# Causal attention on one core: the row maxima of two heads run in the two halves of TensorE's rows, the scores in three single PSUM banks, one exponential per head, 19 loads per unit

## The chip, the cores and the metric

The kernel runs on one NeuronCore of a Trainium2 chip. The metric is the device time in microseconds (us) of one execution of the whole program. PE is TensorE, PEld its weight loads, DVE VectorE, ACT ScalarE, POOL GpSimd, and SP (SPq for its queue) the engine that issues the transfers.

## The reference

The program is a chain of four layers on x of shape 8 x 1024 x 256, each of the form x = x + layernorm(f(layernorm(x))). The change touches the first, causal attention with 16 heads of width 16:

```python
c_q = x @ W_dq;   Q = (c_q @ W_uq).reshape(Bx, Sx, 16, 16)
c_kv = x @ W_dkv; K = (c_kv @ W_uk)...; V = (c_kv @ W_uv)...
scores = einsum('bqhd,bkhd->bhqk', Q, K) / sqrt(16)
attn = softmax(where(causal, scores, -inf), axis=-1)
out = einsum('bhqk,bkhd->bqhd', attn, V).reshape(Bx, Sx, 256) @ W_o
```

The layers behind it are a feed-forward layer with ternary weights, a linear attention that squares its scores (in this kernel the same function as the first, with other settings) and a ternary projection.

## The kernel before, in words

The passes run one after the other: weights, latent (norm, projections, Q, K and V to DRAM), attend with softmax (tiles named `a_`), mix, feed-forward, features, attend without softmax (tiles named `b_`), mix, ternary. Each pass has one program per engine, and every engine works its own program off in order.

**Operands.** Q and K are kept in fp32 accuracy as three bf16 parts each. A head has only 16 features, so `unit_operands` stacks six products of parts along the contraction: 96 rows (`STACK`), in which q holds parts 0,0,0,1,1,2 and k parts 0,1,2,0,1,0. Two more rows (96 and 97) hold minus the row maximum of the scores in two bf16 parts in q, and ones in k. A matmul over 98 rows so gives scores less their maximum. `set_rows` fills rows 96 to 127 once on POOL before the loads. Seven transfers load a unit: q and k for each of the three groups of parts (48, 32 and 16 rows of 8 KB), and v.

**Units.** A unit is 4 heads of one batch entry, 32 units in all. Operands of three units are held (`RING`); the tiles of the first are `first_q`, `first_k` and `first_v`, loaded during the latent pass. Unit n has ten steps: pieces of 512 columns of transposed scores (keys on the partitions), 4608 columns a head. In step s, PE computes for the four heads the scores of step s + 2 (`scores`, line 993), which ACT turns into weights (line 896), POOL masks on the diagonal (line 869), and `weigh` (line 1009) multiplies with v in fp32, four heads side by side in four groups of 32 columns of the array.

**Maxima.** Row maxima are needed before the scores, one unit ahead. PE computes the same scores the other way round (queries on the partitions, `maximum_scores`, line 982) in 36 chunks of 512 columns per unit, each in one PSUM bank; DVE reduces each chunk (line 945 whole, or line 947 with the causal mask). After the last chunk `largest` (lines 953 to 961) turns the maxima into rows, and SP copies them with 8 transfers into the q tile (line 818). In unit n, chunks 16 to 35 of unit n + 1 and then chunks 0 to 15 of unit n + 2 are computed; the first of unit n + 2 waits until all its operands are loaded.

**PSUM.** There are eight banks: 0 to 3 for scores, as two pairs; one exponential of 128 x 1024 covers the two heads of a pair. Banks 4 to 6 take maximum chunks, each free again when DVE has read it. Bank 7 takes the weighted sums.

**Order.** PE's order in a full step is written out: scores of heads 0 and 1, one chunk of maxima, scores of heads 2 and 3, two chunks, `weigh`, one chunk. In steps 2 and 9 (256 columns) it is one chunk after each pair of scores. SP's order in a unit: load of unit n + 2 (released when all weighing of unit n - 1 is done), store of half 0, the rows of maxima of unit n + 1, store of half 1.

Of the kernel before, what the change touches and what calls it, by code (L numbers as in the profile page):

```python
# [35 lines left out]
P = 128  # L36
# [4 lines left out]

STACK = 16 * 6


# [433 lines left out]
def latent_pass(nc, z, m, first):  # L478
    G, DC, GROUPS = z.G, z.DC, z.TILES // z.G
    with ExitStack() as ctx:  # L480
# [18 lines left out]
        @block.sync  # L499
        def _(sp):  # L500
            for u in range(2):
                sp.sem_inc(stored[u], STORED)

            def store(i, u):
                n = 2 * i + u
                sp.wait_ge(vx_ready, 2 * n + 3)
                for t in range(G):
                    sp.dma_start(m.v_dram[bass.ts(i, z.UPB), :, u * G + t, :].rearrange("g p k -> p g k"),
                                 vx[u][:, t, :, :].rearrange("p (g h) k -> p g (h k)", g=z.UPB)).then_inc(stored[u], 16)
                sp.wait_ge(low_done, n + 3)  # L510
# [6 lines left out]
            sp.wait_ge(first_set, 2)  # L517
            for dst, src in unit_operands(z, m, *first, 0):
# [4 lines left out]
            sp.wait_ge(first_loaded, 16 * 7)  # L523
            for u in range(2):
                sp.wait_ge(stored[u], STORED * (GROUPS // 2 + 1))
# [160 lines left out]
def unit_operands(z, m, q_tile, k_tile, v_tile, n):  # L686

    width = z.HPU * z.S
    q, k = [tile[:, :, :].rearrange("p h t -> p (h t)") for tile in (q_tile, k_tile)]
    parts = [m.qk_dram[:, which, bass.ts(n, z.HPU * z.DK), :].rearrange("g (d h) t -> d g (h t)", h=z.HPU)  # L690
             for which in range(2)]
    pairs, row = [], 0
    for q_part, groups in ((0, 3), (1, 2), (2, 1)):
        into = slice(row, row + z.DK * groups)
        q_rows = parts[0][:, q_part:q_part + 1, :]
        pairs.append((q[into, :], q_rows.to_broadcast([z.DK, groups, width]) if groups > 1 else q_rows))
        pairs.append((k[into, :], parts[1][:, 0:groups, :]))
        row += z.DK * groups
    pairs.append((v_tile[:, :, :], m.v_dram[bass.ts(n, 1), :, :, :].rearrange("n p k c -> p (n k) c")))
    return pairs  # L700
# [4 lines left out]
def attend_pass(nc, z, m, first, softmax):  # L705
# [5 lines left out]
    RING = 3  # L711
# [16 lines left out]
    AHEAD = 2  # L728
    PAIRS = 2 if softmax else 3
    SLOTS = 5  # L730
    assert STEPS % SLOTS == 0 and 2 * RING * STEPS % PAIRS == 0

# [11 lines left out]
    assert sum(map(sum, MOST)) == CH  # L744
    with ExitStack() as ctx:
# [15 lines left out]
        st_ready, p_ready, masked, pv_done, o_taken = sm("st_ready", "p_ready", "masked", "pv_done", "o_taken")  # L761
        LOADED = 16 * 7
        STORED = 16
        SB, OB = 4, (7 if softmax else 6, 7)
        OT = len(set(OB))
        PV, PR, STK, DR = SLOTS, PAIRS, SRING, 2
        if softmax:
# [15 lines left out]

        OPERAND = slice(0, STACK + 2 if softmax else STACK)

# [4 lines left out]
        def score_bank(r, s, hd):  # L790
            return 2 * ((2 * (STEPS * r + s) + hd // 2) % PAIRS) + hd % 2

# [9 lines left out]
        def _(sp):  # L802
# [3 lines left out]
            def load(n, r):  # L806
                if softmax:
                    sp.wait_ge(rows_set, 2 * n if isinstance(n, int) and n < RING else 2 * (RING - 1))
                pairs = unit_operands(z, m, qs[r], ks[r], vs[r], n)
                for dst, src in pairs:  # L810
                    sp.dma_start(dst, src).then_inc(loaded[r], 16)

            def load_rows(n, r):
                sp.wait_ge(rows_ready, n + 1)
                for k in range(2):
                    at = qs[r][STACK + k:STACK + k + 1, :, :].rearrange("o h (q b i) -> o (h q) b i", b=4, i=32)
                    for b in range(4):
                        sp.dma_start(at[:, :, b, :], rows[32 * b:32 * b + 32, k, :]).then_inc(rows_loaded, 16)
# [28 lines left out]
        def _(pool):  # L847
# [5 lines left out]
            if first:  # L853
                pool.wait_ge(bias_ready, 1)
                for r in range(1, RING):
                    set_rows(pool, qs[r], ks[r], rows_set, 2 * (r - 1))

            def unit(n, r, rnd, ahead, far):
                for s in range(STEPS):
                    if not DIAG[s]:  # L860
                        continue
                    if not softmax:
                        pool.wait_ge(d_ready, STEPS * n + s + 1 + DR)
                    wait_alone(pool, p_ready, 2 * STEPS * n + 2 * s + 2 + PR, m.alone)
                    for k, at in enumerate(DIAG[s]):
# [9 lines left out]
        def _(act):  # L875
# [13 lines left out]
            def weights(n, r, s):  # L889
                cols = slice(live_from(s), 512)  # L890
                act.wait_ge(pv_done, STEPS * n + s + 1)
                for k in range(2):
                    act.wait_ge(st_ready, 2 * STEPS * n + 2 * s + k + 1)
                    heads = 2 if softmax or k == 0 else 1
                    at = score_bank(r, s, 2 * k)
                    act.activation(p[s % SLOTS][:, 2 * k:2 * k + heads, cols], m.psum[:, at:at + heads, cols],  # L896
                                   ACT.Exp if softmax else ACT.Square, scale=z.DK ** -0.5).then_inc(p_ready, 1)
# [77 lines left out]
        def _(pe):  # L975
            pe.sem_inc(pv_done, PV)
            def maximum_scores(n, r, a, b):
                for c in range(a, b):
                    hd, pieces = chunks[c // 2][0] + c % 2 * HPU // 2, chunks[c // 2][1]
                    pe.wait_ge(s_taken, CH * n + c + 1)  # L980
                    for qt, h, at, w in pieces:
                        last = pe.matmul(m.bank[SB + c % SRING][:, at:at + w], qs[r][0:STACK, hd, qt * P:(qt + 1) * P],  # L982
                                         ks[r][0:STACK, hd, h * 512:h * 512 + w], start=True, stop=True)
                    last.then_inc(s_ready, 1)

            def scores(n, r, s, k):
                h, pieces = steps[s]
                pe.wait_ge(p_ready, 2 * STEPS * n + 2 * s + k + 1)
                if not softmax and k == 0:
                    pe.wait_ge(d_ready, STEPS * n + s + 1)  # L990
                for hd in (2 * k, 2 * k + 1):
                    for kt, at, q, w in pieces:
# [5 lines left out]
            def weigh(n, r, s):  # L998
                h, pieces = steps[s]
                pe.wait_ge(p_ready, 2 * STEPS * n + 2 * s + 2 + PR)  # L1000
                if not softmax:
# [17 lines left out]
            def unit(n, r, rnd, ahead, far):  # L1019
                def some_maxima(first, count):  # L1020

                    if not softmax:
                        return
                    late = CH - 2 * EARLY
                    for k in range(first, first + count):
                        if k < late and ahead:
                            maximum_scores(n + 1, (r + 1) % RING, 2 * EARLY + k, 2 * EARLY + k + 1)
                        if k >= late and far:
                            if k == late:
                                pe.wait_ge(loaded[(r + 2) % RING], LOADED * (rnd + (r + 2) // RING) + LOADED)  # L1030
                            maximum_scores(n + 2, (r + 2) % RING, k - late, k - late + 1)

                dealt = 0
                for s in range(STEPS):
# [4 lines left out]
                    at = (n, r, t) if t < STEPS else (n + 1, (r + 1) % RING, t - STEPS)  # L1039
                    for k in range(3):  # L1040
                        if k == 2:
                            weigh(n, r, s)
                        elif there:
                            scores(*at, k)
                        some_maxima(dealt, MOST[s][k])
                        dealt += MOST[s][k]

            if softmax:
                pe.wait_ge(loaded[0], LOADED)
                maximum_scores(0, 0, 0, CH)  # L1050
                pe.wait_ge(loaded[1], LOADED)
                maximum_scores(1, 1, 0, 2 * EARLY)
            operands(0, 0, 0)
            for s in range(AHEAD):
                for k in range(2):
                    scores(0, 0, s, k)
# [801 lines left out]
```

## Time and profile before

| | |
|---|---|
| median of 3 runs | 2884.16 us (2873.43 to 2885.13) |
| profiled execution | 2883.56 us |
| its span | 2881.8 us |
| PE busy | 2467.9 us, 86% |
| DVE busy | 2230.5 us, 77% |
| ACT busy | 1759.3 us, 61% |
| POOL busy | 562.9 us, 20% |
| mean granted clock of PE | 0.945 |

The span is the time from the first to the last instruction that the profile shows. Busy shares are means over all passes. Matmul records carry a start and a modelled end, so that neighbours overlap; the distance between starts is the safer reading.

### The profile page before, as it was taken

How to read it: one execution, taken by the hardware profiler on the slowest of the kernel's cores; microseconds unless marked ns; L12 is line 12 of the kernel's file. 1: busy time of each engine (PE TensorE's matmuls, PEld its weight loads, DVE VectorE, ACT ScalarE, POOL GpSimd, SP SyncE). 2: the span in 40 equal slices, each digit the busy share in tenths (PEclk: the TensorE clock that was granted, in tenths of full speed). 3: DMA queues.
4: the chain of work that ended last, by engine and by line, in shares of the span. 5: the costliest groups of instructions: out<-in, count | busy, mean ns of one | idle time of the engine just before them, and what ended most of it. 6: DMA issues, size and time to landing. Idle time of an engine off the chain costs nothing. (4 is left out here: it accounts for less than half of the span.)

```text
span 2881.8 us, 57144 instructions
## 1 busy us (share of the span) xinstructions
PE 2467.9 (86%) x15239; PEld 1169.6 (41%) x15239; DVE 2230.5 (77%) x5755; ACT 1759.3 (61%) x2682; POOL 562.9 (20%) x644
## 2 busy tenths in 40 slices
PE   3687999999999999677999997994899999996656
PEld 1342333333333333254666664552233333333544
DVE  4887889999899899286777767995566666666968
ACT  0442566666666666415777756883678778873446
POOL 0344111121111112140000000222222222222200
PEclk9897899999999999898999998997899999998879
DMA  5497353545445353260000002556777777754403
GB/s 173 151 282 209 71 104 80 110 84 100 92 91 101 82 110 77 79 184 1 0 0 0 0 0 69 181 181 175 146 143 145 146 146 146 146 117 132 127 0 117
DMA packets 223820, 309.47 MB, mean 107 GB/s; under 512 B 32321, under 2 KB 170257, under 8 KB 211473
## 3 DMA queue, kind: packets, MB, share of 16 engines
q1 hardware_dynamic: 223472, 307.47, 44.3%
q10 hardware_dynamic: 288, 1.31, 0.3%
q8 instruction: 25, 0.41, 0.1%
q14 instruction: 35, 0.28, 0.0%
HBM read 181.29 MB, written 126.88 MB: 107 GB/s over the span
## 5 line engine op out<-in xcount | busy, mean ns | idle before, releaser
L896 ACT ACTIVATE a_p<-psum 128x1024 f32<-128x1024 f32 (+1 forms) x640 | 567.4, 941 | 305.5 <-PE psum L993 305.3
L896 ACT ACTIVATE b_p<-psum 128x512 f32<-128x512 f32 (+2 forms) x640 | 444.1, 749 | 157.5 <-PE psum L993 154.5
L947 DVE CUSTOM_DVE_ANT_0 a_dump<-psum,a_bias 128x128 bf16<-128x128 f32 (+3 forms) x1024 | 447.7, 488 | 62.3 <-PE psum L982 52.5
L945 DVE TENSOR_REDUCE a_peak<-psum 128x1 f32<-128x512 f32 x512 | 334.3, 687 | 23.1 <-PE psum L982 19.8
L993 PE MATMUL psum<-b_qs,b_ks 96*128 96x512 bf16 (+3 forms) x1536 | 307.2, 330 | 40.9 <-DMA b_vs<-values 40.9
L924 DVE COPY b_twin<-psum 128x512 f32<-128x512 f32 (+1 forms) x320 | 203.9, 637 | 177.0 <-PE psum L993 173.6
L1009 PE MATMUL psum<-b_p,b_vs 128*32 128x512 f32 (+3 forms) x3072 | 314.7, 497 | 6.3 <-POOL b_p L869 6.3
L869 POOL TENSOR_SCALAR_AFFINE_SELECT a_p<-a_p 128x512 f32<-128x512 f32 x256 | 162.5, 635 | 755.4 <-ACT a_p L896 743.7
L982 PE MATMUL psum<-a_ks,a_qs 96*128 96x128 bf16 (+2 forms) x1008 | 275.5, 334 | 27.8 <-DMA a_vs<-values 20.2
L869 POOL TENSOR_SCALAR_AFFINE_SELECT b_p<-b_p 128x512 f32<-128x512 f32 x256 | 159.5, 635 | 453.3 <-DVE b_p L927 442.9
L993 PE MATMUL psum<-a_qs,a_ks 98*128 98x512 bf16 x1008 | 234.4, 328 | 9.1 <-issue 3.6
L993 PEld LDWEIGHTS psum<-b_qs,b_ks 96*128 96x128 bf16 x1536 | 115.1, 98 | 303.4 <-issue 168.8
L927 DVE SCALAR_TENSOR_TENSOR b_p<-psum,b_twin 128x512 f32<-128x512 f32 (+1 forms) x320 | 204.3, 639 | 33.3
L1465 PE MATMUL psum<-f_xt,w_fc 128*128 128x512 f32 x512 | 224.9, 597 | 3.3 <-ACT f_hid L1406 2.8
L1009 PE MATMUL psum<-a_p,a_vs 128*32 128x512 f32 x2016 | 205.8, 496 | 0.5 <-POOL a_p L869 0.3
L1604 POOL TENSOR_TENSOR g_parts<-g_rest,g_parts 128x2048 bf16<-128x2048 f32 x16 | 66.2, 4134 | 639.5 <-DVE g_parts L1592 639.5
L1267 PE MATMUL psum<-wo,m_att 128*128 128x256 f32 x512 | 136.3, 427 | 62.3 <-POOL m_att L1214 39.4
L982 PEld LDWEIGHTS psum<-a_ks,a_qs 96*128 96x128 bf16 x1008 | 84.7, 97 | 224.6 <-DVE a_peak L947 118.1
L982 PE MATMUL psum<-first_k,first_q 96*128 96x128 bf16 (+3 forms) x528 | 150.1, 344 | 25.1 <-SPq L834 12.2
L1476 PE MATMUL psum<-w_proj,f_parts 128*128 128x256 bf16 x1536 | 170.3, 273 | 1.4 <-DVE f_scaled L1354 1.4
L1476 PEld LDWEIGHTS psum<-w_proj,f_parts 128*128 128x128 bf16 x1536 | 150.2, 98 | 19.4 <-DVE f_scaled L1354 1.7
L1343 DVE TENSOR_TENSOR f_rest<-f_sq,f_parts 128x512 f32<-128x512 f32 x128 | 88.5, 691 | 76.9 <-ACT f_sq L1414 75.8
(197 smaller groups left out, 3693.1 us busy)
## 6 DMA issues: line engine op xcount, KB each, us to landing
qk_parts<-l_parts SPq DMA_DIRECT2D x96, 256.0 KB, 3.1
qk_parts<-g_parts SPq DMA_DIRECT2D x96, 256.0 KB, 2.8
values<-l_vx SPq DMA_DIRECT2D x64, 256.0 KB, 3.3
sums<-a_osb SPq DMA_DIRECT2D x64, 256.0 KB, 2.1
m_num<-sums SPq DMA_DIRECT2D x64, 256.0 KB, 3.8
m_inv<-reciprocals SPq DMA_DIRECT2D x64, 256.0 KB, 4.4
values<-g_vx SPq DMA_DIRECT2D x64, 256.0 KB, 3.0
sums<-b_osb SPq DMA_DIRECT2D x64, 256.0 KB, 2.1
```

Of the source, the lines that this page charges most:

```text
L869: pool.affine_select(out=diag, in_=diag, compare_op=ALU.is_ge, fill=0.0, base=0, pattern=[[0, HPU], [1, P]], channel_multiplier=-1).then_i ...
L896: act.activation(p[s % SLOTS][:, 2 * k:2 * k + heads, cols], m.psum[:, at:at + heads, cols], ACT.Exp if softmax else ACT.Square, scale=z.D ...
L924: dve.tensor_copy(twin[s % 2][:, cols], bank).then_inc(twin_ready, 1)
L927: dve.scalar_tensor_tensor(out=p[s % SLOTS][:, 3, cols], in0=bank, scalar=1.0 / z.DK, in1=twin[s % 2][:, cols], op0=ALU.mult, op1=ALU.mult ...
L945: last = dve.tensor_reduce(dst, piece, AX.X, ALU.max)
L947: last = dve.tensor_tensor_reduce(dump[c % SRING][:, at:at + w], piece, bias[:, 512 - w:], 1.0, NEG, ALU.add, ALU.max, dst)
L982: last = pe.matmul(m.bank[SB + c % SRING][:, at:at + w], qs[r][0:STACK, hd, qt * P:(qt + 1) * P], ks[r][0:STACK, hd, h * 512:h * 512 + w], ...
L993: last = pe.matmul(m.bank[score_bank(r, s, hd)][:, at:at + w], ks[r][OPERAND, hd, kt * P:(kt + 1) * P], qs[r][OPERAND, hd, h * 512 + q:h * ...
L1009: last = pe.matmul(m.bank[OB[h]][32 * hd:32 * hd + 32, q:q + w], vs[r][:, kt, 32 * hd:32 * hd + 32], p[s % SLOTS][:, hd, at:at + w], start ...
L1267: last = pe.matmul(bank, att[u][:, c, t * P:(t + 1) * P], wo[:, c, :], start=(c == 0), stop=(c == DC - 1))
L1465: last = pe.matmul(m.bank[F0 + j % 4], m.w_fc[:, c, j * P:(j + 1) * P], xt[u][:, c, :], start=(c == 0), stop=(c == DC - 1))
L1476: last = pe.matmul(bank, parts[u][:, part, j, t * P:(t + 1) * P], m.w_proj[:, j, :], start=(part == j == 0), stop=(part == PARTS - 1 and j ...
```

## The change

- Loads: heads 0 and 1 (the first half of each tile) and heads 2 and 3 (the second half) are loaded apart, in 4 KB rows, 8 + 10 + 1 = 19 transfers per unit. The first half lies on rows 0 to 95, the second on rows 16 to 111 in another order of the products. The rows of minus the maximum move to 112 and 113, and scores run over 114 rows. POOL sets rows 0 to 31 of the second half too: four fills per tile pair where there were two. `first` is loaded in the latent pass in the same 19 transfers.
- Maxima: a head's maximum is taken from four of the six products (for the second half three and a remainder on rows 64 to 111). A head of the first half uses rows 0 to 63 of the array, one of the second rows 64 to 111. For each piece a matmul of one and a matmul of the other follow each other, into two banks. A pair waits until both its banks are read. There are four banks (3 to 6) for maxima.
- Scores: one bank a head, three in all (0 to 2), and one exponential of 128 x 512 per head, 40 per unit where there were 20.
- Order of PE in a full step: scores 0, a pair of maxima, scores 1, `weigh`, a pair, scores 2, scores 3. In steps 2 and 9 the second pair is left out.

```diff
+MAIN = 16 * 4
+TOP = 16 * 7
...
+            for dst, src in unit_operands(z, m, *first, 0, 2, True):
...
+    low, second = slice(0, MAIN // 2), slice(q.shape[1] // 2, q.shape[1])
...
+    eng.memset(q[low, second, :], 0.0).then_inc(step, 1)
+    eng.wait_ge(step, done + 3)
+    eng.memset(k[low, second, :], 1.0).then_inc(step, 1)
...
+LOWER = ((0, 0, 3), (1, 0, 1), (1, 1, 1), (2, 0, 1))
+UPPER = ((2, 0, 1), (1, 1, 1), (0, 2, 1), (0, 0, 2), (1, 0, 1))
...
+        row = TOP - STACK if apart and half else 0
+        for q_part, k_part, groups in (LOWER, UPPER)[half] if apart else SHARED:
+            into = slice(row, row + z.DK * groups)
+            q_rows = parts[0][:, q_part:q_part + 1, :]
+            pairs.append((q[into, :], q_rows.to_broadcast([z.DK, groups, heads * z.S]) if groups > 1 else q_rows))
+            pairs.append((k[into, :], parts[1][:, k_part:k_part + groups, :]))
+            row += z.DK * groups
...
-    PAIRS = 2 if softmax else 3
+    WIDE = 1 if softmax else 2
+    PER = HPU // WIDE
+    SCORES = 3
...
-    SRING = 3
+    SRING = 4
...
-    MOST = [(1, 1, 0) if s in LAST else (1, 2, 1) for s in range(STEPS)]
+    MOST = [(1, 0) if s in LAST else (1, 1) for s in range(STEPS)]
...
+                for j in range(a, b):
+                    hd, pieces = chunks[j]
+                    pe.wait_ge(s_taken, CH * n + 2 * j + 2)
                     for qt, h, at, w in pieces:
+                        for half, rows_of in enumerate((slice(0, MAIN), slice(MAIN, TOP))):
+                            last = pe.matmul(m.bank[SB + (2 * j + half) % SRING][:, at:at + w],
+                                             qs[r][rows_of, hd + 2 * half, qt * P:(qt + 1) * P],
+                                             ks[r][rows_of, hd + 2 * half, h * 512:h * 512 + w], start=True, stop=True)
...
+                    if there:
+                        scores(*at, 0)
+                    some_maxima(dealt)
+                    if there:
+                        scores(*at, 1)
+                    weigh(n, r, s)
+                    if MOST[s][1]:
+                        some_maxima(dealt + 1)
+                    for k in (2, 3):
+                        if there:
                             scores(*at, k)
```

The attend pass without softmax keeps its pairs of banks, its seven loads and its order.

## Rows read from the trace of the kernel before

**Rows 1.** Busy time of each engine in one stretch of the softmax attend pass

```profile
600.00:800.00 200.00, 188.45 (x1359) 69.15 (x1357) 181.01 (x600) 131.11 (x156) 36.21 (x57) 1.00 0.47 96
```

**Rows 2.** Timeline of PE in one unit: start, length, what, count

```profile
701.14 0.39 PE L982 MATMUL psum<-first_k,first_q 96*128 96x128 bf16 x2
...
703.99 0.39 PE L982 MATMUL psum<-first_k,first_q 96*128 96x256 bf16 x2
...
704.65 0.38 PE L982 MATMUL psum<-first_k,first_q 96*128 96x512 bf16 x1
704.87 0.59 PE L993 MATMUL psum<-a_qs,a_ks 98*128 98x512 bf16 x2
705.30 0.38 PE L982 MATMUL psum<-first_k,first_q 96*128 96x512 bf16 x1
705.62 0.64 PE L1009 MATMUL psum<-a_p,a_vs 128*32 128x256 f32 x8
706.19 0.60 PE L993 MATMUL psum<-a_qs,a_ks 98*128 98x512 bf16 x2
...
712.97 0.38 PE L982 MATMUL psum<-first_k,first_q 96*128 96x512 bf16 x1
714.15 0.39 PE L982 MATMUL psum<-a_ks,a_qs 96*128 96x128 bf16 x2 [0.80 <-DMA a_vs<-values]
```

**Rows 3.** Groups of DVE by shape, 263 to 1165 us, all 32 units

```profile
L945 DVE TENSOR_REDUCE a_peak<-psum 128x1 f32<-128x512 f32 x512 | 334.3, 687 | 23.1 <-PE psum L982 19.8
L947 DVE CUSTOM_DVE_ANT_0 a_dump<-psum,a_bias 128x512 bf16<-128x512 f32 x256 | 169.5, 689 | 20.9 <-PE psum L982 20.7
L947 DVE CUSTOM_DVE_ANT_0 a_dump<-psum,a_bias 128x384 bf16<-128x384 f32 x256 | 141.5, 553 | 0.0
L947 DVE CUSTOM_DVE_ANT_0 a_dump<-psum,a_bias 128x256 bf16<-128x256 f32 x256 | 97.9, 421 | 8.0 <-PE psum L982 5.3
...
L947 DVE CUSTOM_DVE_ANT_0 a_dump<-psum,a_bias 128x128 bf16<-128x128 f32 x256 | 73.8, 288 | 33.4 <-PE psum L982 26.5 <-POOL a_bias L851 1.0
```

**Rows 4.** Timeline of DVE around the end of a unit's maxima

```profile
686.24 0.22 DVE L953 TENSOR_REDUCE a_npeak<-a_peak 128x32 f32<-128x64 f32 x1
...
687.65 0.29 DVE L947 CUSTOM_DVE_ANT_0 a_dump<-psum,a_bias 128x128 bf16<-128x128 f32 x1
...
714.27 0.22 DVE L953 TENSOR_REDUCE a_npeak<-a_peak 128x32 f32<-128x64 f32 x1
```

**Rows 5.** Waits, 600 to 800 us: us in total, times, longest

```profile
PEld psum L982 <- DVE a_peak L947: 38.3, 56, 2.1
...
DVE a_dump L947 <- PE psum L982: 10.3, 29, 0.7
...
PE psum L982 <- DMA a_vs<-values: 4.6, 4, 1.6
```

**Rows 6.** Groups by shape, 600 to 800 us: ACT's 128 x 512

```profile
L896 ACT ACTIVATE a_p<-psum 128x512 f32<-128x512 f32 x28 | 15.3, 609 | 5.4 <-PE psum L993 5.4
```

**Rows 7.** Timeline of ACT: two pair exponentials back to back

```profile
704.85 1.94 ACT L896 ACTIVATE a_p<-psum 128x1024 f32<-128x1024 f32 x2 [0.91 <-PE psum L993]
```

**Rows 8.** Timeline of SP: first two and last two of a unit's loads

```profile
700.69 0.63 SPq L811 DMA_DIRECT2D a_qs<-qk_parts  x1
701.51 0.61 SPq L811 DMA_DIRECT2D a_ks<-qk_parts  x1
...
704.25 0.37 SPq L811 DMA_DIRECT2D a_ks<-qk_parts  x1
704.81 0.35 SPq L811 DMA_DIRECT2D a_vs<-values  x1
```

**Rows 9.** Transfers by line: count, KB each, median us from issue to landing

```profile
sums<-a_osb SPq DMA_DIRECT2D x64, 256.0 KB, 2.1
```

**Rows 10.** Line 682 on POOL: ns shortest, median and longest, first and last start

```profile
L682 POOL MEMSET a_ks<- x2: 3506/3506/3506, 267.3 to 274.5; 32x4096 bf16 x2
```

**Rows 11.** Timeline of ACT in the latent pass, behind the load of `first`

```profile
161.91 2.06 ACT L595 ACTIVATE l_parts<-psum 128x512 bf16<-128x512 f32 x4 [4.96 <-DMA qk_parts<-l_parts]
```

More of the change, by code:

```diff
@@ L516, in _ @@
                 sp.wait_ge(stored[u], STORED * 2)
-            sp.wait_ge(first_set, 2)
-            for dst, src in unit_operands(z, m, *first, 0):
+            sp.wait_ge(first_set, 4)
+            for dst, src in unit_operands(z, m, *first, 0, 2, True):
                 sp.dma_start(dst, src).then_inc(first_loaded, 16)
@@ L683, in set_rows, with unit_operands @@
     eng.wait_ge(step, done + 2)
[L686 to L698, printed above, removed]
+    eng.memset(q[low, second, :], 0.0).then_inc(step, 1)
+    eng.wait_ge(step, done + 3)
+    eng.memset(k[low, second, :], 1.0).then_inc(step, 1)
+    eng.wait_ge(step, done + 4)
+SHARED = ((0, 0, 3), (1, 0, 2), (2, 0, 1))
+LOWER = ((0, 0, 3), (1, 0, 1), (1, 1, 1), (2, 0, 1))
+UPPER = ((2, 0, 1), (1, 1, 1), (0, 2, 1), (0, 0, 2), (1, 0, 1))
+def unit_operands(z, m, q_tile, k_tile, v_tile, n, halves=1, apart=False):
+    heads = z.HPU // halves
+    pairs = []
+    for half in range(halves):
+        q, k = [tile[:, half * heads:(half + 1) * heads, :].rearrange("p h t -> p (h t)") for tile in (q_tile, k_tile)]
+        parts = [m.qk_dram[:, which, bass.ts(n, z.HPU * z.DK), :].rearrange("g (d x h) t -> d g x (h t)", x=halves,
+                                                                         h=heads)[:, :, half, :] for which in range(2)]
+        row = TOP - STACK if apart and half else 0
[5 more added lines that the diff above has]
+            row += z.DK * groups
     pairs.append((v_tile[:, :, :], m.v_dram[bass.ts(n, 1), :, :, :].rearrange("n p k c -> p (n k) c")))
@@ L807, in load @@
                 if softmax:
-                    sp.wait_ge(rows_set, 2 * n if isinstance(n, int) and n < RING else 2 * (RING - 1))
-                pairs = unit_operands(z, m, qs[r], ks[r], vs[r], n)
+                    sp.wait_ge(rows_set, 4 * n if isinstance(n, int) and n < RING else 4 * (RING - 1))
+                pairs = unit_operands(z, m, qs[r], ks[r], vs[r], n, *((2, True) if softmax else ()))
                 for dst, src in pairs:
@@ L863, in unit @@
                         pool.wait_ge(d_ready, STEPS * n + s + 1 + DR)
[L864 removed]
+                    wait_alone(pool, p_ready, PER * STEPS * n + PER * s + PER + PR, m.alone)
                     for k, at in enumerate(DIAG[s]):
@@ L891, in weights @@
                 act.wait_ge(pv_done, STEPS * n + s + 1)
[L892 to L896, printed above, removed]
+                for k in range(PER):
+                    act.wait_ge(st_ready, PER * STEPS * n + PER * s + k + 1)
+                    heads = WIDE if softmax or k == 0 else 1
+                    at = score_bank(r, s, WIDE * k)
+                    act.activation(p[s % SLOTS][:, WIDE * k:WIDE * k + heads, cols], m.psum[:, at:at + heads, cols],
                                    ACT.Exp if softmax else ACT.Square, scale=z.DK ** -0.5).then_inc(p_ready, 1)
@@ L1019, in unit, with some_maxima @@
             def unit(n, r, rnd, ahead, far):
[L1020 to L1031, printed above, removed]
+                def some_maxima(j):
+                    late = CP - EARLY
+                    if j < late and ahead:
+                        maximum_scores(n + 1, (r + 1) % RING, EARLY + j, EARLY + j + 1)
+                    if j >= late and far:
+                        if j == late:
+                            pe.wait_ge(loaded[(r + 2) % RING], LOADED * (rnd + (r + 2) // RING) + LOADED)
+                        maximum_scores(n + 2, (r + 2) % RING, j - late, j - late + 1)
                 dealt = 0
@@ L1039, in unit @@
                     at = (n, r, t) if t < STEPS else (n + 1, (r + 1) % RING, t - STEPS)
[L1040 to L1043, printed above, removed]
+                    if not softmax:
+                        for k in range(PER):
+                            if there:
+                                scores(*at, k)
+                        weigh(n, r, s)
+                        continue
+                    if there:
[3 more added lines that the diff above has]
+                        scores(*at, 1)
+                    weigh(n, r, s)
+                    if MOST[s][1]:
+                        some_maxima(dealt + 1)
+                    for k in (2, 3):
+                        if there:
                             scores(*at, k)
-                        some_maxima(dealt, MOST[s][k])
-                        dealt += MOST[s][k]
+                    dealt += sum(MOST[s])
             if softmax:
                 pe.wait_ge(loaded[0], LOADED)
-                maximum_scores(0, 0, 0, CH)
+                maximum_scores(0, 0, 0, CP)
                 pe.wait_ge(loaded[1], LOADED)
-                maximum_scores(1, 1, 0, 2 * EARLY)
+                maximum_scores(1, 1, 0, EARLY)
             operands(0, 0, 0)
             for s in range(AHEAD):
-                for k in range(2):
+                for k in range(PER):
                     scores(0, 0, s, k)
```

34 lines of the change are left out of this document (15 added, 19 removed).

## The prediction, made before the changed kernel ran

> **What bounds the kernel now.** I read the page first: PE is busy for 86% of the span, DVE for 77%, ACT for 61%. These are means over nine passes, so I cut out the pass that the change touches. In 200 us of it PE is busy for 188.45 us, DVE for 181.01, ACT for 131.11, at a granted clock of 1.00 (2.4 GHz) and a DMA share of 0.47 [rows 1]. Two engines are nearly full there, and modelled ends make a busy PE look fuller than it is, so I went on by starts. In the timeline of PE [rows 2] one chunk of maxima takes 0.22 us from start to start (704.65 to 704.87), a full step 2.85 us (701.14 to 703.99), with no gap inside: scores, maxima and weighing follow each other. The reader is to see that PE is dense, and that its density is made of three equal parts: 4608 columns x 4 heads each for maxima and scores, and the weighing, whose four heads run side by side but pass four times.
>
> Then DVE. From the starts of the same kind in the timeline a whole chunk costs about 0.65 us, the masked pieces some 0.08 us less than their durations of 0.689, 0.553, 0.421 and 0.288 [rows 3]: 16 x 0.65 + 8 x (0.61 + 0.475 + 0.345 + 0.21) = 23.5 us a unit. The end of a unit's maxima costs 1.4 us more (686.24 to 687.65) [rows 4], and I add 0.5 us for the end of the loop, an estimate: about 25.4 us. The period of a unit is 714.27 - 686.24 = 28.03 us [rows 4]. So PE has to wait a little for DVE (38.3 us of weight loads held in seven units, most of it behind running matmuls, so hidden), DVE a little for PE (10.3 us), and once a unit PE waits for the last load: 4 times 4.6 us together [rows 5], and in the timeline 714.15 - 712.97 - 0.22 = 0.96 us [rows 2]. PE's own work is then about 28.03 - 0.96 = 27.1 us, of which about 1.2 us is short waits for DVE: 25.9 us packed.
>
> **The change part by part, for one unit of 28.03 us.**
>
> *Maxima side by side.* A matmul of a first-half head on rows 0 to 63 and one of a second-half head on rows 64 to 111 go to different banks. If they run together, half of 18,432 columns goes: 9,216 x 0.215/512 = 3.9 us off PE. The nearest row is the weighing, where eight instructions of 256 columns, in four column groups, take 0.57 us and not four times that (705.62 to 706.19) [rows 2]; but those are column groups. Bounds: 0 (they run one after the other) and -3.9. I take -3.9, since the weighing is the row that it is nearest to.
>
> *Changes of the array's shape.* From a maximum chunk into the weighing the start comes 0.32 us later (705.30 to 705.62) where 0.22 is usual: 0.10 us. Out of it, 0.57 us for 256 columns at four passes of 0.107 leave 0.14 us [rows 2]. Before there are 2 such changes a step, 20 a unit. After, with maxima in half rows, the order scores, maxima, scores, weighing, maxima, scores has 5 in a full step and 4 in steps 2 and 9: 48. That is 28 more. Bounds: 0 (a change of rows may cost nothing; no row shows one) and 28 x 0.14 = 3.9 us, which eats the whole gain. I take 0.10, the entry: +2.8 us. The Trainium skill says it of tiling in general (TensorEngine Tiling (Array Packing), Key Properties): changing the tiling mode, not merely the tile, drains the engine. It gives no price; by that rule the lower bound of 0 falls away, by the rows both ends stay open, and this is the rule that speaks against the change.
>
> *Scores in single banks.* Bank k is free when the exponential of three scores earlier has ended. The critical one is scores 1, which waits for scores 2, three before it: matmul 0.38, exponential 0.609 [rows 6], two handovers of about 0.05, so 1.09 us. The way of PE between them is 3 x 0.215 + 0.22 + 2 x 0.10 = 1.07 us. They meet; I put +0.1 us a unit. If the changes are free, the way is 0.87 and this wait gives back 0.2 us of each full step, 1.6 us a unit: a cheap change is then worth less.
>
> *Forty exponentials.* Two of 128 x 1024 back to back take 1.94 us, so 0.92 each from start to start; four halves start every 0.48 us at best (0.609 less the same overlap), 0.08 us more a step, and at worst 4 x 0.609 = 2.44 [rows 6, 7]. ACT goes from some 17.5 to 18.4 us, at worst 24, of 28: hidden under PE. If that cover goes, it is the bound only below 24 us.
>
> *19 loads.* SP issues the 48-row transfers 0.82 us apart and the 16-row ones 0.56 (704.25 to 704.81) [rows 8]. Two of 48 rows, fourteen of 16 and two of 32 (between, 0.7) take 1.6 + 7.8 + 1.4 = 10.8 us before v is issued, where it is 4.1 us now (700.69 to 704.81). But v now lands at 714.1, 13.4 us after the first issue, so it waits behind 1.5 MB. A transfer of 256 KB that stands alone lands in 2.1 us [rows 9]; 512 KB behind little then takes 3 to 4 us, which gives 13.8 to 14.8 us. PE asks later than now, behind the weighing of step 5: 5 steps of about 2.7 and one of 1.5, less 0.85, is 14.2 us after the unit's start, with the first issue 1.3 us after it. Wait 0.9 to 1.9 us where it was 0.96: bounds 0 and +1.0, I take +0.1, because SP's rate (64 KB in 0.56 us) is below what the engines move and leaves no queue. The eight row transfers and the stores stand behind 11 us of issue, with the rows wanted 14 us after the start: covered.
>
> *DVE.* Its work stays 25.4 us. A pair of banks is released together, so DVE has between one and two pairs (1.3 to 2.5 us) in hand, about as now. With PE at 25.9 - 3.9 + 2.8 + 0.1 = 24.9 us both are equal, and each delay of one shows at the other. The short waits were 1.2 us at 25.9 against 25.4; I take 1.2 + 0.3.
>
> Sum: -3.9 + 2.8 + 0.1 + 0.1 + 0.3 = -0.6 us; without the loss to the meeting of both, -0.9. I take -0.8 us for each of the 30 units with maxima beside them: -24 us.
>
> *Ahead of the units.* POOL fills 3.5 us more per tile pair (two halves of 3.506 us) [rows 10]; in the latent pass POOL is idle then, at the start of attend the load of unit 1 begins 3.5 us later, and its 19 issues add up to 3. DVE works on the 36 chunks of unit 0 meanwhile: +0 to 5, I take 2. In the latent pass SP's issues of `first` hold its stores 6.7 us longer. ACT already waits 4.96 us for a store behind that load [rows 11]; the queues drain while SP issues, so +0 to 7, I take 2. Together +4.
>
> Forecast: 2883.6 - 24 + 4 = 2863.6, say 2862 us. The profiled execution is 0.6 us under the median, so that the two are the same base. A difference of 0.5% (14.4 us) is about what a measurement of this kernel can tell from none.
>
> **The rivals.**
>
> *Changes are nearly free, DVE bounds.* PE falls to 22.1 us plus 1.6 for the exponentials; DVE's 25.4 us with 1 us of friction gives 26.4 a unit: -1.6 x 30 + 4 = -44, 2840 us. For it: both switches in the rows also change the data type and the column groups, a change of rows alone may be less. Against: the drain is that of the array itself.
>
> *The load holds the unit.* If 4 KB rows move no faster and v lands 16 us after the first issue, PE waits 3 us in each unit, 2 more than now: -0.8 + 2 - 0.6 (DVE's waits fall into it) = +0.6, so 2883.6 + 18 + 4 = 2906 us. It decides from 15.4 us of landing on. Against: issue, not bandwidth, sets the pace.
>
> *The two halves do not overlap.* PE keeps 25.9, gains 2.8 us of changes: 28.8 with its waits at least 29.8 a unit, +1.8 x 30 + 4: 2940 us. It decides when less than 0.8 of 3.9 us overlaps. For it: no row has two row groups at work. By the Trainium skill (TensorE: Matmul & The Clock Gate, Part 3) matmuls in distinct row groups run concurrently; no run here shows that yet.
>
> *The gain just covers the costs.* Changes at 0.13 us and load at its upper bound: within 15 us of before, 2880 us.
>
> **How the numbers follow.** Forecast 0.38 (2848 to 2874), free changes 0.24, costs cover the gain 0.18, load 0.10, no overlap 0.10. Faster by over 0.5% (under 2869.7): three quarters of the first and the second, 0.53, and a little of the last but two, 0.55; within: 0.22; slower: 0.23. The range 2828 to 2908 leaves out the no-overlap case, and some at each end.
>
> **What would show it.** In PE's timeline of the changed kernel: two maximum matmuls starting a few ns apart, the next 0.22 us on (right) or each 0.22 us (wrong); starts from scores 0 into a maximum chunk 0.32 us apart, or 0.22; a wait of scores 1 for ACT; the period between two starts of line 953's counterpart, forecast 27.2 us; the wait on v at half of each unit near 1 us. In the latent pass the wait of ACT for its store, 5 to 7 us. The forecast is wrong if the period stays near 28, or falls to 26.4.

## The result, and the profile after

The changed kernel takes 2898.16 us in the median of 7 runs (2891.59 to 2904.92), the kernel before beside it 2885.04 us (2870.02 to 2888.19). The ratio is 1.0057, interval 1.0033 to 1.0081: slower by 13 us. I had forecast 2862 us, a gain of some 22 us. The profiled execution took 2904.92 us.

The same stretch of the softmax attend pass as [rows 1], of the kernel after (columns: length, busy of PE, PEld, DVE, ACT, POOL, granted clock, DMA share, GB/s):

```profile
600.00:800.00 200.00, 181.30 (x1370) 53.91 (x1366) 172.78 (x599) 140.86 (x298) 35.53 (x56) 1.00 0.47 95
```

PE and DVE are both less busy than before (188.45 and 181.01) and neither is full: both wait more than before. The clock is the same. The unit is only 0.2 us longer (below), so DVE's smaller share is mostly less work: between 400 and 1050 us DVE is busy for 25.4 us a unit before and 24.4 after. Whole chunks that come as a pair start 0.60 us apart where 0.65 was usual, and the end of a unit's maxima takes 1.04 us where it took 1.4. That last difference comes from one operation (line 957, now 973): 0.55 us before, while a mask of POOL runs beside it, and 0.19 after, when POOL stands still.

The timeline of PE in one unit of the kernel after (start, length, what, count):

```profile
722.56 0.39 PE L999 MATMUL psum<-first_k,first_q 64*128 64x512 bf16 x2
722.88 0.39 PE L1012 MATMUL psum<-a_qs,a_ks 114*128 114x512 bf16 x1
723.20 1.06 PE L1028 MATMUL psum<-a_p,a_vs 128*32 128x512 f32 x8
724.97 0.39 PE L999 MATMUL psum<-a_ks,a_qs 64*128 64x128 bf16 x4 [0.70 <-DMA a_vs<-values]
...
731.87 0.39 PE L1012 MATMUL psum<-first_q,first_k 114*128 114x512 bf16 x1 [0.84 <-DMA first_q<-a_rows]
...
733.84 0.39 PE L999 MATMUL psum<-a_ks,a_qs 64*128 64x512 bf16 x2
734.16 0.82 PE L1012 MATMUL psum<-first_q,first_k 114*128 114x512 bf16 x4
734.91 0.39 PE L999 MATMUL psum<-a_ks,a_qs 64*128 64x512 bf16 x2
735.24 0.39 PE L1012 MATMUL psum<-first_q,first_k 114*128 114x384 bf16 x2
735.56 0.64 PE L1028 MATMUL psum<-a_p,a_vs 128*32 128x256 f32 x8
736.13 0.86 PE L1012 MATMUL psum<-first_q,first_k 114*128 114x384 bf16 x5
736.92 0.39 PE L999 MATMUL psum<-a_ks,a_qs 64*128 64x512 bf16 x2
737.24 0.28 PE L1012 MATMUL psum<-first_q,first_k 114*128 114x256 bf16 x1
738.19 1.07 PE L1028 MATMUL psum<-a_p,first_v 128*32 128x512 f32 x8 [0.66 <-ACT a_osb L903]
```

Three things stand in it against [rows 2]. Two maximum matmuls of 512 columns (x2) are over in 0.39 us, the length of one, and the scores follow 0.32 us after their start: a pair costs what one cost, plus 0.10 us. That 0.10 us stands at each change of the array's shape (733.84 to 734.16, 722.88 to 723.20). And there are waits: 0.66 us of the weighing for ACT's copy of the sums, which was not there before, and 0.84 us of the first scores of a unit for the rows of the maxima, which was 0.3 us at most.

The waits of the kernel after, 600 to 800 us, beside [rows 5]:

```profile
PEld psum L999 <- DVE a_peak L963: 39.9, 46, 2.1
...
DVE a_dump L963 <- PE psum L999: 15.2, 24, 1.0
PEld psum L1028 <- ACT a_osb L903: 11.1, 14, 0.9
...
DVE a_peak L961 <- PE psum L999: 10.0, 25, 0.6
PE psum L1028 <- ACT a_osb L903: 7.7, 14, 0.7
...
PE psum L999 <- DMA a_vs<-values: 3.8, 4, 1.2
...
PE psum L1012 <- DMA a_qs<-a_rows: 2.3, 3, 0.9
```

The wait on `a_osb` comes 14 times in seven units, twice a unit. From the starts it is 738.19 - 737.24 - 0.21 = 0.74 us before a unit's first weighing, and 0.51 us before its fourth: 1.25 us.

ACT at the first of these places, in the kernel after:

```profile
734.59 3.06 ACT L912 ACTIVATE a_p<-psum 128x512 f32<-128x512 f32 x6 [1.05 <-PE psum L1012]
737.53 0.60 ACT L903 ACTIVATE a_osb<-psum 128x512 f32<-128x512 f32 x1
738.01 0.68 ACT L912 ACTIVATE a_p<-psum 128x256 f32<-128x256 f32 x2
```

The last weighing of the unit is over at 736.13, when PE goes on to scores 2. The copy stands in ACT's program behind the four exponentials of that step, and scores 2 and 3 of the step are now issued behind the weighing. So ACT can't copy before it has had scores 2 and 3: 737.53, where behind the weighing alone it could start at about 736.2 (an estimate from the weighing's end). Bank 7 is the only one for sums, and the next weighing (738.19) needs it. Before, all four scores of a step stood ahead of the weighing, and the copy was next for ACT when the weighing ended.

The period of a unit by DVE's last operation on the maxima (first and last start; before, then after in a fence of its own):

```profile
L961 DVE STREAM_TRANSPOSE a_rows<-a_split x24: 245/245/246, 405.2 to 1053.4; 128x64 bf16<-128x64 bf16 x24
```

```profile
L977 DVE STREAM_TRANSPOSE a_rows<-a_split x23: 245/245/246, 411.9 to 1036.3; 128x64 bf16<-128x64 bf16 x23
```

(1053.4 - 405.2) / 23 = 28.18 us before, (1036.3 - 411.9) / 22 = 28.38 us after. These are means. In both profiles the granted clock falls to its lower level, 0.50 (1.2 GHz), for 3.4 us in two of the thirty units, and such a unit takes 29.5 to 29.7 us; in the changed kernel it does so for 6.8 us in one more, which takes 32.1 us. The median unit is 28.03 us before and 28.27 after.

**Where the 14 us are.** In the two profiles the last instruction on a tile of the softmax attend pass starts at 1196.9 and 1211.3 us: +14.4, about the whole difference of the medians (13.1). 2.9 us come ahead of the pass (first maximum matmul at 263.1 and 266.0), 9.6 us in the thirty units with maxima (845.0 and 854.6 us from the second unit's rows to the last; 30 x 0.24 = 7 us by the median units, the rest is the clock), 2.3 us behind them, and 0.4 us are won between the first maxima and the second unit's rows. The 7 us by which the profiled execution is slower beyond that stand in the mix pass, whose code is the same, and the medians don't show them.

### The profile page after: what moved, and what is told of

It reads as the page before. It is cut to its first block and busy times, and to the rows that moved or that the text cites. A ratio compares the mean times of both kernels' runs of the same rounds, so it can differ in the third digit from the quotient of the medians.

```text
span 2903.2 us, 59404 instructions
## 1 busy us (share of the span) xinstructions
PE 2424.2 (83%) x15239; PEld 1097.5 (38%) x15239; DVE 2206.8 (76%) x5755; ACT 1806.5 (62%) x3322; POOL 572.6 (20%) x650
## 5 line engine op out<-in xcount | busy, mean ns | idle before, releaser
L912 ACT ACTIVATE a_p<-psum 128x512 f32<-128x512 f32 (+1 forms) x1280 | 614.4, 560 | 269.5 <-PE psum L1012 268.1
L963 DVE CUSTOM_DVE_ANT_0 a_dump<-psum,a_bias 128x128 bf16<-128x128 f32 (+3 forms) x1024 | 437.5, 486 | 82.2 <-PE psum L999 79.7
L961 DVE TENSOR_REDUCE a_peak<-psum 128x1 f32<-128x512 f32 x512 | 323.1, 684 | 44.8 <-PE psum L999 44.1
L1012 PE MATMUL psum<-a_qs,a_ks 114*128 114x512 bf16 x1008 | 246.6, 332 | 15.6 <-DMA a_qs<-a_rows 8.6
L999 PE MATMUL psum<-a_ks,a_qs 64*128 64x128 bf16 (+2 forms) x1008 | 150.6, 337 | 28.5 <-DMA a_vs<-values 23.6
L1294 PEld LDWEIGHTS psum<-wo,m_att 128*128 128x128 f32 x512 | 111.9, 223 | 95.8 <-DVE x L1202 36.2
L1492 PEld LDWEIGHTS psum<-f_xt,w_fc 128*128 128x128 f32 x512 | 97.2, 192 | 122.9 <-issue 112.7
```

Of the source, the lines that this page charges most:

```text
L912: act.activation(p[s % SLOTS][:, WIDE * k:WIDE * k + heads, cols], m.psum[:, at:at + heads, cols], ACT.Exp if softmax else ACT.Square, sca ...
L961: last = dve.tensor_reduce(dst, piece, AX.X, ALU.max)
L963: last = dve.tensor_tensor_reduce(dump[c % SRING][:, at:at + w], piece, bias[:, 512 - w:], 1.0, NEG, ALU.add, ALU.max, dst)
L999: last = pe.matmul(m.bank[SB + (2 * j + half) % SRING][:, at:at + w], qs[r][rows_of, hd + 2 * half, qt * P:(qt + 1) * P], ks[r][rows_of, h ...
L1012: last = pe.matmul(m.bank[score_bank(r, s, hd)][:, at:at + w], ks[r][OPERAND, hd, kt * P:(kt + 1) * P], qs[r][OPERAND, hd, h * 512 + q:h * ...
L1294: last = pe.matmul(bank, att[u][:, c, t * P:(t + 1) * P], wo[:, c, :], start=(c == 0), stop=(c == DC - 1))
```

## The experiments

Each ran beside the kernel before, whose medians there are 2880.5 to 2882.9 us (2885.04 beside the changed kernel); so two runs of this table are compared by their ratios as well as by their times. Times are medians; periods are means from the same line of DVE between 400 and 1060 us (28.18 us for the kernel before). By median units e1 is at 27.80 us, e4 at 28.28, e6 at 27.81: the clock is in the means of e4 and e6.

| run | time, us | ratio to before, interval | period, us |
|---|---|---|---|
| changed | 2898.16 | 1.0057, 1.0033 to 1.0081 | 28.38 |
| e1_sums_between | 2878.62 | 0.9997, 0.9982 to 1.0013 | 27.82 |
| e2_before_single_banks | 2944.26 | 1.0214, 1.0186 to 1.0242 | 30.05 |
| e3_before_split_loads | 2884.28 | 1.0003, 0.9986 to 1.0020 | 28.03 |
| e4_v_apart | 2895.40 | 1.0049, 1.0032 to 1.0066 | 28.50 |
| e5_ahead_9 | 2851.36 | 0.9880, 0.9849 to 0.9911 | 26.86 |
| e6_ahead_10 | 2888.87 | 1.0018, 1.0005 to 1.0030 | 28.07 |
| e7_before_v_apart_9 | 2851.31 | 0.9888, 0.9868 to 0.9908 | 27.17 |
| e8_ahead_7 | 2982.59 | 1.0355, 1.0333 to 1.0377 | 31.23 |
| e9_ahead_9_sums_last | 2875.81 | 0.9991, 0.9973 to 1.0008 | 27.72 |
| e10_pair_between_scores | 2858.90 | 0.9927, 0.9899 to 0.9955 | 27.11 |

**The sums between the exponentials.**

```diff
                 for k in range(PER):
+                    if k == PER // 2 and between:
+                        between()
                     act.wait_ge(st_ready, PER * STEPS * n + PER * s + k + 1)
...
-                    if s == LAST[0]:
-                        take_sums(n, 0)
-                take_sums(n, 1)
+                    sums = (lambda: take_sums(n, LAST.index(s))) if s in LAST else None
+                    inner = sums if softmax else None
```

> The changed kernel with one move in ACT's program: the copy of the weighted sums stands between the second and the third exponential of a step, not behind all four. First theory (the new wait of the weighing on that copy, 0.73 and 0.51 us a unit, is time of the unit): the period of a unit falls from 28.3-28.5 us to about 27.3, and the whole by 25 to 37 us. Rival (something else holds the unit, the maxima on DVE or the load, and takes the slack): the wait on the copy vanishes from the trace, the period stays within 0.3 us, the whole within 9 us.

2878.62 us: 19.5 us less than the changed kernel (17 by the ratios), and level with before. The wait on `a_osb` is gone from the list. The period fell by 0.56 us (0.47 by median units), between the two branches of the expectation and less than half of the 1.25 us that were freed. The waits of e1, 600 to 800 us:

```profile
PEld psum L1015 <- ACT a_p L914: 45.1, 120, 1.5
...
PE psum L1015 <- DMA a_qs<-a_rows: 5.6, 5, 1.3
```

The first scores of a unit wait longer for the rows of the maxima than in the changed kernel (2.3, 3 times), and the last load is waited for less (0.2 us a unit, by starts, where it was 1.0). The rest of the 1.25 us has a plainer answer in the trace. By starts (each distance between two starts of PE less the shortest that this pair of shapes shows) PE now waits 0.78 us a unit before scores 1, for ACT's exponential of scores 2, and it does so exactly twice a unit, in the steps in which the copy stands between the exponentials. One such place, in e5 (further below), which has the same order on ACT; first ACT, then PE:

```profile
716.47 0.63 ACT L906 ACTIVATE a_osb<-psum 128x512 f32<-128x512 f32 x1
716.95 2.12 ACT L917 ACTIVATE a_p<-psum 128x512 f32<-128x512 f32 x4
```

```profile
717.65 0.39 PE L1018 MATMUL psum<-first_q,first_k 114*128 114x512 bf16 x1 [0.27 <-ACT a_p L917]
```

The copy takes 0.48 us of ACT (716.47 to 716.95), the exponential of scores 2 comes so much later, and with three banks scores 1 needs its bank. So 1.25 us of waits became 0.78, a gain of 0.47, which is what the median unit fell by. One cause is shown, the place of the copy, and its size is enough for the loss of 13 us against before. It is not enough for the 36 us between forecast and result.

**Single banks alone, on the kernel before.** `WIDE = 1`, `SCORES = 3`, and the order kept: scores 0 and 1, a chunk, scores 2 and 3, two chunks, weighing.

> The kernel before with only one part of the change: scores in three single banks and one exponential a head; order of PE, maxima, loads as before. If the three single banks are dear by themselves (the ring: a score waits for the exponential three before it), each step waits about 0.2 us and the whole is 40 to 60 us slower. If they cost nothing by themselves (first theory: their cost in the changed kernel comes from the order, scores 2 and 3 behind the weighing), it is within 15 us of the kernel before.

2944.26 us, 63 us slower, 1.9 us a unit. In the old order scores 3 follow soon on scores 0, whose exponential they wait for. Its waits, 600 to 800 us:

```profile
PEld psum L995 <- ACT a_p L898: 40.4, 81, 0.8
...
PE psum L995 <- ACT a_p L898: 5.0, 14, 0.4
```

My first theory was wrong here: in the old order the three banks are dear by themselves. In the changed kernel they are not, and I put that down to scores 2 and 3 behind the weighing; no run has the new order without the other parts. The same order makes the copy of the sums late.

**Split loads alone, on the kernel before.** Each load by halves of the heads, both on rows 0 to 95: 13 transfers.

> The kernel before with the loads alone split by halves of the heads: 13 transfers a unit with rows of 4 KB in place of 7 with rows of 8 KB; all else as before. If the load of a unit is held by SP's rate of issue, v lands 1 to 2 us later, the wait of PE for v grows from about 1 to 2 or 3 us a unit, and the whole is 30 to 60 us slower. If bytes set it (first theory, since v's wait stayed at 1 us in the changed kernel), within 10 us of before, with up to 3 us lost in the latent pass.

No difference (2884.28 us). Rows of 4 KB in 13 transfers cost nothing in the units; the 19 of the change were not run alone. The waits for v even fell, from 20.9 to 6.4 us between 400 and 1050 us, and the median unit stayed at 28.0 us: in the kernel before that wait was not what held the unit.

**v on a semaphore of its own.**

```diff
-        LOADED = 16 * (19 if softmax else 7)
+        LOADED = 16 * (18 if softmax else 7)
+        v_loaded = sm(*[f"v_loaded{r}" for r in range(RING)])
...
+                    pe.wait_ge(v_loaded[r], 16 * rnd + 16)
                     pe.wait_ge(rows_loaded, ROWS_LOADED * n + ROWS_LOADED)
```

> The changed kernel with v counted on a semaphore of its own, for which PE waits only before the unit's first scores: the maxima two units ahead no longer wait for v. If the wait for v (about 1 us a unit) is on the path, the period falls by 0.5 to 1 us and the whole by 15 to 30 us; if DVE is then not ready either, the wait turns into one for DVE and the whole falls by under 9 us.

2895.40 us, its interval overlaps that of the changed kernel. The wait for v is gone, and the wait for the rows took its place: 29.3 us between 400 and 1050 us (two rows of the list, 20.4 and 8.9) where the changed kernel has 9.5 (6.3 and 3.2). Neither branch of the expectation named that, and it gave the next theory.

**A ring through the maxima.** In the unit of the changed kernel above: the first scores of a unit at 703.59, as at 731.87 a period later; the last pair of the next unit's maxima at 722.56; then, in the timelines of DVE and of SP's queue:

```profile
724.56 0.22 DVE L969 TENSOR_REDUCE a_npeak<-a_peak 128x32 f32<-128x64 f32 x1
725.33 0.24 DVE L977 STREAM_TRANSPOSE a_rows<-a_split 128x64 bf16<-128x64 bf16 x1
```

```profile
725.60 4.99 SPq L834 DMA_DIRECT2D first_q<-a_rows  x8
```

and the scores at 731.87. PE 18.97 us, DVE 3.04, transfers 6.27: together 28.28 us, the unit. Three stretches between four points always add up; what makes a ring of them is that each waits for the one before. The rows are issued as soon as DVE has them, the last of the eight lands 6.1 us after the first is issued, and the scores start 0.12 us behind that. DVE is not idle before the last pair either: it is still reading the pair before it, for which it had waited 0.23 us. In the kernel before the same points are these (PE, SP's queue, PE), with the last chunk at 712.97 [rows 2]:

```profile
693.91 0.60 PE L993 MATMUL psum<-a_qs,a_ks 98*128 98x512 bf16 x2
```

```profile
715.68 4.99 SPq L818 DMA_DIRECT2D first_q<-a_rows  x8
```

```profile
721.95 0.60 PE L993 MATMUL psum<-first_q,first_k 98*128 98x512 bf16 x2 [0.30 <-DMA first_q<-a_rows]
```

PE 19.06 us, DVE 2.71, transfers 6.27. The wait for v lies between the last maxima and the scores, beside DVE and the transfers and not in front of them; that is why e3 and e4 gained nothing when it shrank. To shorten the ring, the last maxima of a unit must be computed earlier in the unit before: `EARLY`, the pairs done two units ahead, was 8.

> The changed kernel with the sums between the exponentials, v on its own semaphore, and 9 in place of 8 pairs of maxima computed two units ahead, so that a unit's last pair of maxima, and with it the transfer of the maxima, comes one pair earlier. Theory: the ring last pair of maxima, DVE's end work, eight row transfers (7 us from their first issue to landing), scores of the next unit, holds the unit at 27.8 us. Then the period falls by up to one slot, 1.0 to 1.4 us, until DVE's 25.4 us or the load hold it: 26.6 to 27.2 us, the whole 2845 to 2862 us, and PE's wait for the rows falls from 1.2 us a unit to under 0.4. Rival (DVE or PE holds it, or the operands of two units ahead are not there yet): the wait for the rows turns into one for q and k or for DVE, the whole stays within 9 us of 2878.

> As the one before with 10 pairs two units ahead. If the ring of the rows held it with 9 too, another 0.5 us a unit; if the load of q and k has become late (asked for 2.4 us earlier than with 8), PE waits for it and the period goes back up by about 1 us, 30 us in the whole.

> The kernel before with v on its own semaphore and 9 (18 chunks) in place of 8 (16 chunks) two units ahead. The ring, worked out from its rows, is 28.1 us long there too. If it holds the kernel before as well, the period falls from 28.17 us to about 27.3 (PE's packed 25.9 us and its waits for DVE stop it there), the whole by 20 to 30 us. If PE alone holds it, it stays within 9 us of before.

> The changed kernel with the sums between the exponentials and 7 in place of 8 pairs two units ahead: the rows come one pair later. If the ring of the rows holds the unit, the period grows by 1.0 to 1.4 us and the whole by 30 to 42 us over 2878. If the load or DVE holds it, the wait for the load (0.2 us a unit there) goes and the whole stays or falls a little.

With 9: 2851.36 us, the period 26.86, and the rows are not in the list of waits. What is left there, 600 to 800 us:

```profile
PEld psum L1018 <- ACT a_p L917: 38.8, 124, 0.7
PEld psum L1005 <- DVE a_peak L969: 30.2, 49, 1.4
...
PE psum L1005 <- DMA a_ks<-qk_parts: 2.4, 4, 0.9
```

With 10 PE asks for q and k before they are there: 37.2 us of waits on them between 400 and 1050 us (25.3 and 11.9; with 9 it was 11.5), period 28.07, as expected. With 7 the period is 31.23, more than the one slot that I gave it: 3.4 us where 1.0 to 1.4 were expected. Its list and its stretch:

```profile
PE psum L1015 <- DMA a_qs<-a_rows: 12.4, 5, 2.5
```

```profile
600.00:800.00 200.00, 171.95 (x1219) 49.95 (x1218) 157.91 (x543) 126.32 (x264) 33.00 (x52) 0.94 0.38 79
```

PE stands still for up to 2.5 us a unit, and the granted clock of the stretch is 0.94, between its two levels of 1.2 and 2.4 GHz, where it was 1.00. Right behind that wait, in every unit, it stands at the lower level for 3.4 us (6.8 in every seventh or so):

```profile
702.40:705.80 3.40, 3.40 (x24) 0.94 (x23) 1.47 (x8) 1.19 (x2) 0.00 (x0) 0.51 0.00 0
```

In the kernel before a unit with one such stretch is 1.7 us longer than one without (29.7 and 28.0). That leaves some 1.7 us of the 3.4 for the slot, an estimate, against 1.0 to 1.4 expected. The direction and the place are those of the ring.

The kernel before with the same two edits takes 2851.31 us: the ring held it too. The two edits were not run apart there, but v's wait alone is ruled out by e3. The changed kernel, with its copy moved, is no faster than the kernel before when both have them (2851.36 and 2851.31 us). The period of the kernel before, 27.17 us, stands 1.3 us over the 25.9 us of PE's packed work, and the changed kernel's 26.86 us 2.0 us over 24.9 us.

**The fourth field.** Ring relaxed (v apart, 9), sums behind all exponentials as the change has them.

> The changed kernel with v apart and 9 pairs two units ahead, but ACT's copy of the sums behind all four exponentials as the change has it. It fills the fourth field beside the changed kernel (period 28.4), the one with the sums between (27.8) and the one with both (26.86). If the wait for the sums (1.25 us a unit) adds to whatever else holds the unit: period 26.86 + 0.6 to 1.25 = 27.5 to 28.1 us, the whole 2870 to 2888 us. If it counts only while the ring of the maxima's rows holds the unit: within 9 us of 2851.

2875.81 us: the copy's place costs 24 us also here (32 by the ratios; 0.86 us a unit). With the ring as it was it cost 19.5 us (17). So the waits of the weighing lie on the path in both cases: they are inside PE's part of the ring, and inside PE's own sum where the ring is relaxed.

**The second pair between scores 2 and 3**, on e5:

```diff
                     weigh(n, r, s)
-                    if MOST[s][1]:
-                        some_maxima(dealt + 1)
-                    for k in (2, 3):
-                        if there:
-                            scores(*at, k)
+                    if there:
+                        scores(*at, 2)
+                    if MOST[s][1]:
+                        some_maxima(dealt + 1)
+                    if there:
+                        scores(*at, 3)
```

> As the run with 9 ahead and the sums between (2851 us), with the second pair of maxima between scores 2 and scores 3 in place of ahead of both. One more change of the array's shape in a full step, 8 a unit at 0.10 us: +0.8 us. PE has then 1.5 us in place of 1.07 between scores 2 and the scores 1 that wait for its exponential, so that the wait there (0.86 us a unit in the run before) goes. If both are time of the unit they cancel: within 9 us of 2851. If the wait there was hidden behind DVE, the whole is 20 to 30 us slower; if the change of shape costs nothing, 20 us faster.

2858.90 us, 7.5 us over e5 by the times and 14 by the ratios (intervals 0.9899 to 0.9955 and 0.9849 to 0.9911, which just overlap), 0.25 us a unit: about the band of "they cancel". But half of the reason given for it did not happen. By starts PE's packed work (waits left out) is 25.7 us a unit where e5 has 24.9: the eight changes cost their 0.8 us. The wait before scores 1 did not go: it is still there twice a unit, 0.58 us where it was 0.78, at the copy again. The rest of what the changes cost was won at other waits.

## Why the prediction was wrong, by its own steps

- **Maxima side by side, -3.9 us: right.** Two matmuls in the length of one. The rival without overlap falls.
- **Changes of the array's shape, +2.8 us: right.** 0.10 us each (0.32 against 0.22), the value taken. The rival with free changes falls; the Trainium skill's rule that a changed tiling mode drains the engine (TensorEngine Tiling (Array Packing), Key Properties) agrees with these rows.
- **Packed work of PE, 24.9 us: right.** Through all starts between 400 and 1050 us, waits left out, the changed kernel has 28.38 - 3.5 = 24.9 us a unit, the kernel before 28.18 - 2.3 = 25.9.
- **Scores in single banks, +0.1 us: near in this order.** Between a pair and scores 1 the starts show 0.11 us a unit, and scores 3 wait another 0.13 us in each of the two short steps. But e2 shows 1.9 us in the old order, and in e1 and e5 the wait before scores 1 is 0.8 us. The prediction's sum for it (exponential and handovers against PE's way) has no copy in it, and the copy is what makes this wait.
- **19 loads: right.** v is issued 10.0 us after the first transfer (10.8 worked out) and PE has it 14.2 us after it (13.8 to 14.8). The rival in which the load holds the unit falls with that; that its 2906 us is the nearest of all to the result is chance, and so is a result inside the range, which reached so far up for its sake. The sentence behind it failed: that the eight row transfers are "covered". I put down when the rows are wanted and that SP is free, not when DVE has them. They land 0.12 us before the first scores start, in nearly every unit of both kernels.
- **Forty exponentials: the step that failed.** I costed them as ACT's busy time, "hidden under PE", and missed what moving scores 2 and 3 behind the weighing does to ACT's order: the copy of the sums comes after them, and one bank of sums makes PE wait 1.25 us a unit. Over thirty units that is about 37 us, the size of the miss of 36. Undoing it alone gives 17 to 19.5 us, because with three banks 0.78 of the 1.25 us comes back before scores 1.
- **DVE, +0.3 us: wrong in kind.** I took DVE's work as 25.4 us in both kernels and the 1.2 us of short waits as friction between two equal engines. DVE has 24.4 us in the changed kernel, and what held the unit was a ring of 28 us through PE, DVE and eight transfers. It gets shorter only by what falls in its parts. PE's part is 19.06 us before, 18.97 in the changed kernel with its copy late, and 18.50 in e1 (691.91 to 710.41); DVE's part, which ends on two chunks now where it ended on one, grew from 2.71 to 3.04 us and took 0.33 back. Of the gain of 1.0 us e1 so kept 0.23 by median units (0.36 by means). The ring is not the whole answer, though: with it relaxed for both, e5 against e7 keeps only 0.31.
- **Ahead of the units, +4 us: the size about right, the source wrong.** 2.9 us, in the latent pass. The prediction let POOL's two more fills cost nothing there. They are most of it. DVE's first operations of the pass (before, then after) end right behind POOL's fills (84.5 us before, 87.8 after), and the same four take 1.38 us when POOL stands still:

```profile
82.05 3.55 DVE L170 TENSOR_SCALAR l_xn<-x,l_mv,l_rs 128x256 f32<-128x256 f32 x4
```

```profile
81.62 6.68 DVE L172 TENSOR_SCALAR l_xn<-x,l_mv,l_rs 128x256 f32<-128x256 f32 x4
86.01 1.83 POOL L689 MEMSET first_k<- 32x2048 bf16 x1
91.88 1.38 DVE L172 TENSOR_SCALAR l_xn<-x,l_mv,l_rs 128x256 f32<-128x256 f32 x4
```

That is 3.1 us, and the load of `first` begins 2.5 us later (143.59 against 141.06). The load itself adds little: SP holds its stores for 10.3 us (143.59 to 153.85), 5.6 more than before, and ACT's wait behind it grew from 4.96 [rows 11] to 5.69 us:

```profile
165.15 2.06 ACT L597 ACTIVATE l_parts<-psum 128x512 bf16<-128x512 f32 x4 [5.69 <-DMA qk_parts<-l_parts]
```

The right sum: -1.0 us of packed work and +1.25 us for the copy, with the other waits as they were (2.3 us a unit before, 3.5 less 1.25 after), are +0.2 us a unit by the periods; over all thirty units of the two profiles it is 0.3 (9.6 us, some 2.5 of it the clock), and with 2.9 ahead, 2.3 behind and 0.4 won at the start the pass shows 14.4 us.

What stays open: e5 has 2.0 us of waits a unit over its packed work and e7 1.3. The 0.8 us before scores 1, which e7 has not, would cover the difference, but no run took them out by themselves. A second bank for the sums, or a copy on another engine, was not tried. A shorter transfer of the rows, from two queues or in fewer pieces, was not tried on the chip.

## What to carry to other kernels

When work moves past a wait on one engine, walk through the programs of the others in their order: what stood behind the moved work there, as here a copy behind two exponentials, moves with it. Before a gain on the busiest engine is counted, close the ring: start at an operand that arrives just in time (a wait of 0.1 to 0.3 us is enough of a sign), go back through who makes it, and see at each stretch that it waits for the one before; if they close after one period, the gain must lie on the ring. Here one pair of maxima more ahead of time, with v counted apart, changes no engine's work; it gave the kernel before 1.1% and the changed one, with its copy moved, 0.9% (2878.62 to 2851.36 us). It was worth more than the change itself, which gave nothing on top of it.

## What was not expected of the hardware

A matmul in 64 rows and one in 48 rows of the array's other half run together at the full rate with no price but 0.10 us at each change between them and matmuls over 114 rows, the same as at a change to four groups of 32 columns (0.10 us, [rows 2]). Eight more such changes a unit put 0.8 us on PE's packed work (e10). And POOL's fills hold up DVE: four operations that take 1.38 us alone took 6.68 us beside them.
